# Cross-attention block: weight norms summed on TensorE, attention and MLP placed up to two slots earlier

## What is computed

```python
q, kv = _ln(queries, q_norm_g, q_norm_b), _ln(tokens, kv_norm_g, kv_norm_b)
qp, kp, vp = q @ Wq.T + bq, kv @ Wk.T + bk, kv @ Wv.T + bv      # in_proj, three thirds
scores = jnp.einsum('bhld,bhtd->bhlt', qh, kh) / np.sqrt(hd)
dist = jnp.sqrt(jnp.maximum(jnp.sum(diff * diff, axis=-1), 0.0))  # query_coords - token_coords
scores = scores - spatial_scale[None, :, None, None] * dist[:, None] + spatial_offset[None, :, None, None]
scores = jnp.where(key_padding[:, None, None, :], -jnp.inf, scores)
attn_out = (softmax(scores) @ vh) @ out_proj_w.T + out_proj_b
x = queries + attn_out
h = jax.nn.gelu(_ln(x, g, b) @ mlp_w1.T + mlp_b1, approximate=False)
x = x + (h @ mlp_w2.T + mlp_b2)
```

## Time and profile before

| | before |
|---|---|
| median of 3 runs | 1246.0 us (1245.63 to 1246.84) |
| profiled execution, its own time | 1247.5 us |
| its span | 1245.7 us |
| TensorE, share of the span | 97% (1207.0 us) |
| VectorE | 80% |
| GpSimd | 80% |
| ScalarE | 69% |
| mean granted TensorE clock | 0.993 |

### The profile page before, as it was taken

The page is one execution under the profiler, slowest core; times in us unless marked ns, Lnnn a source line. Parts: engine busy times, 40 slices in busy tenths (PEclk is TensorE's granted clock), DMA queues, the critical chain, the costliest instruction groups (busy, mean ns, idle before and its releaser), DMA issues.

```text
span 1245.7 us, 27442 instructions
## 1 busy us (share of the span) xinstructions
PE 1207.0 (97%) x9258; PEld 783.0 (63%) x9258; DVE 1001.4 (80%) x2640; ACT 861.4 (69%) x1934; POOL 993.0 (80%) x1286
## 2 busy tenths in 40 slices
PE   7887989999999999999999999999999999999998
PEld 2333556666666666666666666666666676666665
DVE  6798998888888988988888888888798987778321
ACT  6878768776767667776768677776767776676331
POOL 5587888989898998989898988989798987767320
PEclk9999899999999999999999999999999999999999
DMA  8599998999899898989889997989999998768533
GB/s 237 155 200 216 222 220 200 205 193 202 197 204 219 182 212 199 207 188 201 203 203 208 195 220 180 218 183 203 186 212 207 191 219 172 169 174 175 145 111 127
DMA packets 469692, 241.67 MB, mean 194 GB/s; under 512 B 385056, under 2 KB 409904, under 8 KB 469552
## 3 DMA queue, kind: packets, MB, share of 16 engines
q1 hardware_dynamic: 469552, 239.93, 85.5%
HBM read 109.66 MB, written 12.58 MB: 98 GB/s over the span
## 4 chain that ended last, share of the span: by engine, by line
PE 79%; DVE 7%; ACT 4%; SPq 3%; issue 3%; DMA 2%; POOL 2%; POOLq 0%; DVEq 0%; ACTq 0%
PE ps_up L648 25%; PE ps_down L663 25%; PE ps_qk L584 11%; PE ps_vo L608 6%; PE ps_vo L605 5%; PE ps_s L619 4%; PE ps_pv L633 3%; DVE soft L1109 1%; DVE p_nat L1130 1%; DMA stack<-stack 1%; SPq L386 1%; SPq L395 1%; ACT soft L812 1%; DVE x_nat L1086 1%; ACT L843 1%
## 5 line engine op out<-in xcount | busy, mean ns | idle before, releaser
L648 PE MATMUL ps_up<-hT,w 128*128 128x256 f16 x3072 | 377.2, 273 | 0.2 <-ACT u L852 0.2
L663 PE MATMUL ps_down<-w,hid 128*128 128x512 f16 x1536 | 372.8, 379 | 0.5 <-DVE hid L1162 0.4
L1318 POOL TENSOR_SCALAR p_nat<-soft,row_inv 128x256 f16<-128x256 f32 x480 | 315.9, 669 | 55.2 <-DVE row_inv L1120 54.2
L648 PEld LDWEIGHTS ps_up<-hT,w 128*128 128x128 f16 x3072 | 300.3, 98 | 89.4 <-ACT u L852 0.8
L812 ACT ACTIVATE soft<-soft,neg_max 128x256 f32<-128x256 f32 x512 | 255.2, 500 | 124.3 <-DVE neg_max L1109 123.6
L1109 DVE CUSTOM_DVE_ANT_0 soft<-ps_s,soft,factor 128x256 f32<-128x256 f32 x512 | 225.3, 476 | 101.6 <-PE ps_s L619 101.1
L1130 DVE SCALAR_TENSOR_TENSOR p_nat<-soft,row_inv,p_nat 128x256 f16<-128x256 f32 x480 | 284.0, 631 | 1.6 <-POOL p_nat L1318 1.5
L1326 POOL TENSOR_SCALAR soft<-dist,scale_neg,offset 128x512 f32<-128x512 f32 x256 | 242.1, 946 | 23.0 <-DVE p_nat L1126 10.8
L663 PEld LDWEIGHTS ps_down<-w,hid 128*128 128x128 f16 x1536 | 148.6, 97 | 132.2 <-DVE hid L1162 0.9
L852 ACT ACTIVATE u<-ps_up,bias,up_scale 128x256 f32<-128x256 f32 x256 | 142.4, 557 | 110.3 <-PE ps_up L648 109.3
L1334 POOL TENSOR_SCALAR hid<-u,hid_scale 128x1024 f16<-128x1024 f32 x64 | 76.5, 1196 | 104.2 <-ACT u L858 104.2
(11 more groups left out here) (130 smaller groups left out, 1578.3 us busy)
## 6 DMA issues: line engine op xcount, KB each, us to landing
w<-x_scratch SPq DMA_DIRECT2D x256, 256.0 KB, 3.1
stack<-qk_parts SPq DMA_DIRECT2D x256, 96.0 KB
raw<-in_ctx SPq DMA_DIRECT2D x32, 256.0 KB, 3.5
raw<-in_x SPq DMA_DIRECT2D x32, 256.0 KB, 3.1
c_stage<-in_w SPq DMA_DIRECT2D x32, 256.0 KB, 3.9
x<-in_x SPq DMA_DIRECT2D x32, 256.0 KB, 3.5
out<-x SPq DMA_DIRECT2D x32, 256.0 KB, 3.3
tok_rows<-in_tok_xy SPq DMA_DIRECT2D x16, 256.0 KB, 4.6
```

Of the source, the lines that this page charges most:

```text
L648: mm = e.matmul(ps_up[s % 2][:, 0:L], w_1_sb[:, wp, k, m * P:(m + 1) * P], hT[:, b % 2, :, xp * KT + k, :], start=(k, wp, xp) == (0, 0, 0) ...
L663: mm = e.matmul(ps_down[tt][:], hid[:, chunk % HID_RING, i, hp, tt * P:(tt + 1) * P], w_2_sb[:, s % W2_RING, wp, :], start=(m == 0 and (hp ...
L1318: mine = e.tensor_scalar(p_nat[:, nat, HI, lc, :], soft[:, ring, lc, :], row_inv[:, ring, lc:lc + 1], 1.0, ALU.mult, ALU.mult)
```

## The change

1. `weight_sums` is gone. `total(w)` is now four one-column matmuls that accumulate in PSUM (one for V and O), and the matrix on their left is a broadcast column `mix`, which holds the gain and shift terms, in place of ones. A new `column_totals` (slot -32) and `mix_columns` (slot -30, four VectorE operations) make it. `square_norm` is one operation that reads PSUM.
2. `up_scale` and the products for the hidden norm are written once for four chunks.
3. UP 31 → 29 (DOWN 37 → 35), `attend` and the two attention splits one slot earlier, `V_PROJ` (0, 4) → (0, 3), `O_PROJ` (23, 25) → (22, 24), `H_APPLY` (25, 27) → (24, 26), the hidden norm and scales two slots earlier. `V_PROJ`'s and `O_PROJ`'s followers move with them.
4. The 32 weight pieces take 30 slots: at pieces 11 and 24 two are done in one slot (`STEP`).
5. The mask operations move from slot -21 to -5, `small_scale` from -5 to -4, `score_factors` becomes a step of its own.

```diff
-        UP = 31
+        UP = 29
...
+        STEP = tuple(p - (p >= 11) - (p >= 24) for p in range(2 * N_CHUNKS * KT))
...
-        TOTAL = (-30, -28, -4, 0) + tuple(range(0, 32, 4))
-        NORM = (-28, -25, -3, 0) + tuple(range(1, 33, 4))
-        GAIN = (-27, -24, -3, 1) + tuple(range(2, 34, 4))
+        TOTAL = (-30, -28, -4, 0) + tuple(STEP[KT * n + KT - 1] - 3 for n in range(2 * N_CHUNKS))
+        NORM = (-28, -25, -3, 0) + tuple(STEP[KT * n + KT - 1] - 2 for n in range(2 * N_CHUNKS))
+        GAIN = (-27, -24, -3, 1) + tuple(STEP[KT * n + KT - 1] - 1 for n in range(2 * N_CHUNKS))
...
-        V_PROJ, O_PROJ, H_APPLY = (0, 4), (23, 25), (25, 27)
+        V_PROJ, O_PROJ, H_APPLY = (0, 3), (22, 24), (24, 26)
...
             def total(w):
-                gate.wait_ge(s_wsum, WSUM[w])
...
-                part = total_columns(w)
-                e.matmul(ps_tot[:, part], one[:].to_broadcast([P, P]), sums[:, part], start=True, stop=True).then_inc(s_tot)
+                factors = (mix[:, MIX[w]:MIX[w] + 1] if w in MIX else one[:]).to_broadcast([P, P])
...
+                for k in range(parts):
+                    mm = e.matmul(ps_tot[:, of_tensor(w)], factors, squares[:, k:k + 1], start=(k == 0), stop=(k == parts - 1))
+                mm.then_inc(s_tot)
...
-                for G in due(slot, 9, GROUP, N_HG):
+                for G in due(slot, 8, GROUP, N_HG):
                     attend(G)
...
             def square_norm(w):
-                e.tensor_copy(tot[:, part], ps_tot[:, part]).then_inc(s_tsb)
...
-                e.scalar_tensor_tensor(out=mine, in0=square, scalar=tot[:, shift:shift + 1], in1=tot[:, bias:bias + 1],
-                                       op0=ALU.mult, op1=ALU.add).then_inc(s_n2)
...
-                e.scalar_tensor_tensor(out=mine, in0=mine, scalar=1.0 / D, in1=gained, op0=ALU.mult, op1=ALU.add).then_inc(s_n2)
...
-                e.tensor_scalar(mine, mine, TINY, None, ALU.max).then_inc(s_n2)
+                    e.tensor_scalar(mine, square, bias_d[:, bias:bias + 1], TINY, ALU.add, ALU.max).then_inc(s_n2)
...
-                    e.tensor_tensor(hid_norm[:, 0, c:c + 1], mine, norm[:, AT_W1 + c:AT_W1 + c + 1], ALU.mult).then_inc(s_gs)
...
             def hidden_norm():
+                e.tensor_tensor(hid_norm[:, 0, :], norm[:, AT_W2:N_W], norm[:, AT_W1:AT_W2], ALU.mult).then_inc(s_n2)
```

More of the change, by code:

```diff
@@ L508, in sync_program @@
                         h_turn(b, tt)
-                for s in due(slot, 20, ITEM, MT):
-                    store_w2(s)
+                for p in steps_of(slot, 4):
+                    if p >= MT:
+                        store_w2(p - MT)
                 for s in due(slot, DOWN - 2, ITEM, N_STEPS):
@@ L521, in sync_program @@
                         store_out(2 * b + tt)
-                for step in due(slot, -6, ITEM, 2 * N_CHUNKS * KT):
-                    load_chunk(*divmod(step, KT))
+                for p in steps_of(slot, -6):
+                    load_chunk(*divmod(p, KT))
             for ring in range(X1_RING):
@@ L692, in tensor_program @@
                         warm(count)
+                if slot == -32:
+                    column_totals()
                 if -1 <= slot < UP:
@@ L710, in tensor_program @@
                         total(w)
-                for step in due(slot, 1, ITEM, MT):
+                for step in due(slot, 0, ITEM, MT):
                     w1_bias(*divmod(step, CH))
@@ L865, in scalar_program @@
                         qk_hi(G, which)
-                for G in due(slot, 10, GROUP, N_HG):
+                for G in due(slot, 9, GROUP, N_HG):
                     if slot >= UP:
@@ L902, in scalar_program @@
                         dist_square(b, c)
[L903 to L908 removed]
+                for p in steps_of(slot, -4):
+                    chunk_square(*divmod(p, KT))
+                for p in steps_of(slot, 2):
+                    if p < MT:
+                        w1_hi(*divmod(p, KT))
+                    else:
+                        w2_hi(p - MT)
                 for chunk in due(slot, UP + CH - 1, CH, B * N_CHUNKS):
@@ L1222, in vector_program @@
                         qk_lo(G, which)
-                for G in due(slot, 10, GROUP, N_HG):
+                if slot == -4:
+                    small_scale()
+                for G in due(slot, 9, GROUP, N_HG):
                     if slot >= UP:
@@ L1240, in vector_program @@
                         v_lo(b, tt)
-                for step in due(slot, 3, ITEM, MT):
-                    w1_lo(*divmod(step, KT))
-                for s in due(slot, 19, ITEM, MT):
-                    w2_lo(s)
+                for p in steps_of(slot, 3):
+                    if p < MT:
+                        w1_lo(*divmod(p, KT))
+                    else:
+                        w2_lo(p - MT)
                 for i in due(slot, 3, ITEM, N_ITEMS):
```

144 lines of the change are left out of this document (68 added, 76 removed).

## The result

The changed kernel takes 1255.3 us (five runs, 1255.1 to 1257.94) where the kernel before took 1246.0; the ratio is 1.0081, with a 95% interval of 1.007 to 1.0093. It is slower by 9.3 us, where 1244.9 was forecast with a range from 1238 to 1252. Its profiled execution took 1257.9 us with a span of 1256.1, so the two traces, of 1256.1 and 1245.7 us, differ by 10.4.

The account below looks back on a forecast made before the run. VectorE was taken to bound the ramp and TensorE the steady state. The terms -0.9 - 10 + 3.0 + 4 + 2.8 = -1.1 us gave 1246.4 from the profiled 1247.5, so 1244.9 against the median 1246.0; range 1238 to 1252.

Parts of the forecast that it names:

- The steady state: Behind the crossover: h's transpose lands at 13.8 us against 13.47, a 0.3 us wait per batch, 13 times, +4 us.
- the ramp: Slot 1's scores to the crossover: VectorE loses 11.9 us of work, counted at 0.85, crossover 10 us earlier, ends 5 and 13.
- the masks: Preamble: two mask operations leave the place ahead of W_q's low parts, gain 0.9 us, ends 0 and 1.5.
- the return: At the crossover: two slots fewer of scores and projections done, now on TensorE's path, +3.0 us.
- the end: Last two batches, without new scores: TensorE waits 1.3 and 1.5 us for h's transpose, +2.8 us, ends 0 and 4.
- the price of VectorE's time: In the ramp: each microsecond taken off VectorE counts 0.85, so 11.9 us less work gives 10 us.
- 1.9 us of waits: Ramp, L987: waits beside running GpSimd operations would pass to other VectorE operations, so 1.9 us were left out of the gain.
- the second rival: SyncE's queue ahead of L648: h's transpose late by a whole operation in each batch, 0.9 x 13 = 12, 1253; chance 0.20.
- The fourth rival: Ramp: gain is zero because uploads of W1's and W2's pieces set the slots, only losses stay, 1255; chance 0.03.
- the first rival: Steady state: h's transpose lands in time, chain 13.4 us or less, the 4 us go, 1240.5 to 1241; chance 0.27.
- The additional table load a batch: ScalarE, a batch's third quarter: one more table load of 1.28 us beside TensorE, costed at nothing, ends 0 and +2.
- The weight loads of the column totals: TensorE: six more loads per total, 1.1 us, beside fillers; without that cover eight totals cost up to 9 us.

Follow-up runs that it names:

- e2: Changed kernel with the mask operations and the mask's DMA back at their old slots (-21 and -18); 1254.6 us, ratio 1.0075 to the kernel before.
- e4: Kernel before, all slots kept, with norms by column matmuls and one VectorE operation, one up_scale and one set of hidden norms; 1245.9 us, ratio 1.0001.
- e9: e4 with the low parts of p of items 4 to 27 writing only one of two halves; 1244.5 us, ratio 0.9991 to the kernel before.
- e5: Changed kernel with only UP set back to 31 (DOWN = 37); 1246.8 us, ratio 1.0012 to the kernel before.
- e6: Changed kernel with only UP set to 30 (DOWN = 36); 1246.8 us, ratio 1.0 to the kernel before.
- e1: Changed kernel with both two-piece slots in W1 (5 and 11 in place of 11 and 24); 1253.1 us, ratio 1.0054 to the kernel before.
- e7: Changed kernel with UP = 30 and the two-piece slots in W1 (5 and 11); 1244.6 us, ratio 0.9985 to the kernel before.
- e3: Changed kernel with h's low part and h's transpose put ahead of p's, in the same slots; 1256.5 us, ratio 1.008 to the kernel before.
- e8: e3 with four low parts of p per batch writing only one of two halves; 1253.2 us, ratio 1.0059 to the kernel before.

## Why the prediction was wrong

The sum on record was -0.9 - 10 + 3.0 + 4 + 2.8. The traces give, in the same order: nothing (e2), -7.2, and for the last three together 1.8 + 10.9 + 3.1 = 15.8 where 9.8 stood. The steady state failed by 6.9 us (10.9 where 4 stood), the ramp by 2.8, the masks by 0.9; the return and the end came out 0.9 less than forecast, and 1.7 more is the scatter of the profile's start.

**The ramp, 10 us: wrong in its parts.** The step that failed is the price of VectorE's time. The reading was VectorE busy for 0.93 and TensorE waiting 19.7 us for `neg_max`, so 0.85 of every microsecond taken off VectorE was counted. e4 took 8.1 us of such work off, and the time stayed within 1.6 us either way; e9 took another 9 off, and the ramp is the same. `neg_max` was the last wait in a chain, not its cause: VectorE takes its operations in the order of the program, and with less work it stood at ScalarE's `qk_parts` instead. The profile had that row (1.8 us before), and ScalarE's waits show the 7.4 us for the copies that stand behind it; the prediction read neither:

```profile
ACT qk_parts L805 <- DMA stack<-stack: 7.4, 4, 2.0
```

Of the 1.9 us of waits that the prediction let pass to other operations, 1.4 are to be seen in the low part of p and 0.5 in x's, if that rise is what it was taken for.

What shortened the ramp is the two slots that it lost: item 2 to the first W1 product takes 127.9 us with UP = 31 (e5), 123.2 with 30 (e6), 119.2 with 29, about 4.3 each. That is a slot's whole length and not the 2.85 us of VectorE's item work that the prediction counted for one; the two errors, in opposite directions, nearly made up for each other. The place of the pairs took 2 to 3 us of it back (e1 against the changed kernel, e7 against e6), 0.5 to 1.1 us of that where ScalarE waited for W2's stores. This term was missing: the prediction took pieces and slots as a load, and did not ask which ring of buffers has a piece for each of them. It is the one new wait that could be computed from the table of slots alone.

**The steady state, +4: mechanism right, size wrong.** This is the term that was mis-sized the most. The chain for `hT` was right to 0.3 us or better in the batch computed. The changed kernel's VectorE and SyncE in the batch of the earlier trace rows:

```profile
648.78 0.17 DVE L1127 RECIPROCAL row_one<-row_sum 128x4 f32<-128x4 f32 x1
...
649.07 0.75 DVE L1156 SCALAR_TENSOR_TENSOR x<-ps_vo,factor,x 128x512 f32<-128x512 f32 x1
...
650.87 0.87 DVE L1140 SCALAR_TENSOR_TENSOR p_nat<-soft,row_inv,p_nat 128x256 f16<-128x256 f32 x2
...
652.05 1.27 DVE L1172 SCALAR_TENSOR_TENSOR hid<-u,hid_scale,hid 128x1024 f16<-128x1024 f32 x1
...
654.05 1.30 DVE L1140 SCALAR_TENSOR_TENSOR p_nat<-soft,row_inv,p_nat 128x256 f16<-128x256 f32 x2
655.27 1.09 DVE L1100 TENSOR_TENSOR h_nat<-x_n,h_nat 128x512 f16<-128x512 f32 x1
```

```profile
655.38 1.24 SPq L402 DMA_TRANSPOSE pT<-p_nat  x1
656.66 1.33 SPq L430 DMA_TRANSPOSE hT<-h_nat  x1
```

From the block's start at 646.25: inverse at 2.53 (2.53 forecast), residual 2.82 (2.83), low part of p 4.62 (4.63), hidden part 5.80 (5.83), second low part 7.80 (8.1), transpose 10.41 (10.55). What failed is the landing: 3.2 us, the median, was used, where the earlier trace rows had up to 4.5. Batch b begins with product 16 b. Ahead of batches 4, 6 and 10 the transpose held SyncE's queue for 2.04 to 2.10 us (1.3 in the others), the product started 4.1 to 4.2 us behind it and waited 0.9 to 1.0. Ahead of batch 12 it started 4.7 us behind and waited 1.5. Ahead of batches 8 and 13 it was p's transpose in front that held the queue, for 2.13 and 1.89 us where the chain had 1.3, and the waits were 0.9 and 0.7. The kernel before had such transposes too (2.18 us ahead of product 96), and no wait followed there.

Twelve batches lost 10.9 us, 0.9 each. That is the number of the second rival, `hT` late by a whole operation, "price 0.9 x 13", which gave 1253 and had 0.20, but its mechanism, the same delay in each batch, is not what the trace has: the six listed waits for `hT` make 5.8 of the 10.9 us, the waits for score maxima behind the crossover 2.2, and the rest is in delays that the list doesn't show, such as 0.2 us ahead of batches without a listed wait (the product starts 3.87 to 3.94 us behind the one before it, in e3 3.70). The fourth rival's 1255, with 0.03, is nearly the measured time, and that is a coincidence: it had no gain in the ramp, and the ramp gained 7.2 us. Below the wait for `hT` lay a second one of about the same size, for VectorE (e3, e8), so even a chain that lands in time would not have given the first rival's 1240.5.

**The return at the crossover and the end, 3.0 + 2.8.** Measured 1.8 in the first batch and 3.1 from product 208 on. At the end of the first batch stands a wait for `hT` of 1.4 us; TensorE's own busy time in it is 66.3 us where it was 64.9. The waits ahead of the last two batches are 0.3 us each and not 1.3 and 1.5, so most of the 3.1 is work that was owed (TensorE is busy 2.2 us longer from product 208 on). The sum of the two terms came out about right with less wait and more work than it had.

**Costed at nothing.** The additional table load a batch (72 ahead of the exponentials where 59 were) cost nothing that can be found: UP = 30 has the same 72, and loses 1.4 us in the twelve batches. The weight loads of the column totals stayed under the fillers: slots 8 to 25 in e4 are 72.2 against 72.4.

```profile
L671 PE MATMUL ps_up<-hT,w 128*128 128x256 f16 x3072 | 377.1, 273 | 8.0 <-issue 7.8
...
L1140 DVE SCALAR_TENSOR_TENSOR p_nat<-soft,row_inv,p_nat 128x256 f16<-128x256 f32 x480 | 269.5, 601 | 1.9 <-POOL p_nat L1328 1.9
...
L837 ACT ACT_TABLE_LOAD x72 | 92.4, 1283 | 1.3
```

The first row answers to the 3072 products of which the page before had "0.2" of idle time; the second is the low part of p over the whole span, where 631 ns stood before.

## What to carry to other kernels

That an engine is busy for 93% and the bound engine waits for it does not yet show that it holds the stretch: look at what the busy engine itself waits for, and at what that one waits for, and take the load off in one experiment before a sum is made of it. When steps are moved nearer to each other, count each ring of buffers in slots, use the long landing and not the median when the landing is the last link, and look for a second chain whose slack is about as small, since the wait that goes only shows the one beneath.

## What was not expected of the hardware

Transposes by DMA of the same size and form held SyncE's queue for 1.3 us in most batches and for 2.0 to 2.1 in some, and the product that reads them started 3.2 us behind the one kind and 4.1 behind the other. 32 loads issued from ScalarE's queue where SyncE's had issued them cost the kernel 4 to 7 us (medians), though SyncE's queue was relieved of them. And the same instructions took 8.9 us at a granted clock of 1.00 in one profile and 12.4 at 0.59 in another, before the ramp had begun.
